# VectorE scales each image's last projection earlier; two ScalarE steps and one TensorE step change places

## What is computed

```python
xn = (x - mean) / jnp.sqrt(var + EPS) * g + b          # over the 64 channels
q, k, v = split(einsum('bchw,oc->bohw', xn, w_qkv))     # 8 heads of 32
q = q * scale
k = jax.nn.softmax(k, axis=-1)                          # over the 1024 pixels
context = jnp.einsum('bhcn,bhdn->bhcd', k, v)
out = jnp.einsum('bhcd,bhcn->bhdn', context, q)
x1 = einsum('bchw,oc->bohw', out, w_out) + b_out + xn

y = conv3x3(jnp.sign(x1), jnp.sign(W))                  # 64 to 64 channels
yn = (y - mean) * gamma / jnp.sqrt(var + BN_EPS) + beta # over all 8 images
result = yn + x1
```

## Time and profile before

| What | Value |
|---|---|
| median of 3 executions | 112.19 us (112.02 to 114.37) |
| the profiled execution | 112.12 us, its span 109.9 us |
| TensorE matmul busy | 76.6 us (70% of the span) |
| VectorE busy | 62.1 us (56%) |
| ScalarE busy | 53.5 us (49%) |
| GpSimd busy | 37.8 us (34%) |
| chain that ended last | PE 54%, DVE 14%, ACT 13%, issue 12% |
| mean granted TensorE clock | 0.934 of full speed |

### The profile page before, as it was taken

The page is one execution under the profiler, slowest core; times in us unless marked ns, Lnnn a source line. Parts: engine busy times, 40 slices in busy tenths (PEclk is TensorE's granted clock), DMA queues, the critical chain, the costliest instruction groups (busy, mean ns, idle before and its releaser), DMA issues.

```text
span 109.9 us, 2262 instructions
## 1 busy us (share of the span) xinstructions
PE 76.6 (70%) x855; PEld 44.3 (40%) x855; DVE 62.1 (56%) x134; ACT 53.5 (49%) x101; POOL 37.8 (34%) x49
## 2 busy tenths in 40 slices
PE   4999577776993997993980899666967999710000
PEld 4933145433551643553560556434625444310000
DVE  4516845966067148368379526935641629738900
ACT  0436569367577186291690038084171339349400
POOL 6000665602914206708539605706400000004410
PEclk9999999999999999999999679999999999995555
DMA  1999743900592000980002941061070081522893
GB/s 62 221 244 232 155 94 76 210 10 0 113 207 62 6 3 0 197 185 6 0 0 46 208 110 25 0 136 61 0 191 6 0 191 29 121 47 45 234 332 152
DMA packets 7565, 11.03 MB, mean 100 GB/s; under 512 B 1924, under 2 KB 4036, under 8 KB 7556
## 3 DMA queue, kind: packets, MB, share of 16 engines
q1 hardware_dynamic: 6164, 9.33, 37.1%
q0 software_dynamic: 336, 1.05, 2.8%
q10 hardware_dynamic: 1056, 0.52, 2.0%
HBM read 2.51 MB, written 2.10 MB: 42 GB/s over the span
## 4 chain that ended last, share of the span: by engine, by line
PE 54%; DVE 14%; ACT 13%; issue 12%; POOL 1%; ACTq 1%; POOLq 1%; DVEq 0%
PE ps L797 7%; PE ps L700 4%; PE ps L809 4%; PE ps L930 4%; PE ps L889 4%; ACT E L412 4%; PE ps L859 3%; PE ps L776 3%; DVE mx L556 3%; PE ps L878 3%; DVE E_lo L550 3%; DVE XN L537 2%; PE ps L815 2%; ACT lnv L361 2%; ACT rstd L367 2%
## 5 line engine op out<-in xcount | busy, mean ns | idle before, releaser
L556 DVE TENSOR_REDUCE mx<-ps 128x1 bf16<-128x1024 f32 x16 | 19.5, 1222 | 5.5 <-PE ps L754 5.5
L412 ACT ACTIVATE E<-ps 128x512 f32<-128x512 f32 x32 | 17.2, 590 | 4.8 <-PE ps L781 4.8
L309 POOL TENSOR_TENSOR E_lo<-E 128x512 bf16<-128x512 f32 x11 | 12.2, 1121 | 10.8 <-ACT E L412 10.8
L419 ACT COPY PT<-ps 128x256 f32<-128x256 f32 x8 | 3.0, 372 | 24.0 <-PE ps L815 15.6
L293 POOL TENSOR_SCALAR x_hi<-XN,hi_rows 128x512 bf16<-128x512 f32 x7 | 5.4, 766 | 21.2 <-DVE XN L537 21.2
L303 POOL TENSOR_TENSOR x_lo<-XN,x_hi 128x512 bf16<-128x512 f32 x8 | 9.2, 1154 | 9.4 <-DVE x_hi L578 8.9
L776 PE MATMUL ps<-wk_max,x_hi 64*128 64x256 bf16 x64 | 9.1, 275 | 2.4 <-ACT E L412 1.7
L561 DVE SCALAR_TENSOR_TENSOR wk_max<-ps,hi_rows,wk_hi 128x256 bf16<-128x256 f32 x8 | 3.9, 484 | 11.8 <-PE ps L761 11.7
L797 PE MATMUL ps<-E,XT 128*64 128x256 f32 x64 | 7.8, 384 | 3.7 <-issue 3.7
L336 POOL DMA_DIRECT2D out<-OUT x3 | 1.8, 614 | 22.9 <-DVE OUT L688 22.9
L779 PE MATMUL ps<-wk_lo,x_hi 64*128 64x256 bf16 x64 | 8.9, 269 | 0.0
(11 more groups left out here) (142 smaller groups left out, 152.6 us busy)
## 6 DMA issues: line engine op xcount, KB each, us to landing
X<-XN SPq DMA_DIRECT2D x16, 128.0 KB, 2.3
X<-in_x SPq DMA_DIRECT2D x4, 256.0 KB, 5.3
S<-x_hi SPq DMA_DIRECT2D x8, 128.0 KB, 2.4
S<-x_lo SPq DMA_DIRECT2D x8, 128.0 KB, 2.4
X<-X SPq DMA_DIRECT2D x4, 256.0 KB, 3.9
X<-X SPq DMA_DIRECT2D x8, 128.0 KB, 2.4
X<-in_x SPq DMA_DIRECT2D x6, 128.0 KB, 3.4
out<-OUT SPq DMA_DIRECT2D x3, 256.0 KB, 4.3
```

Source lines behind the costliest of these rows:

```text
L309: nc.gpsimd.tensor_tensor(e_lo, e, e_hi, ALU.subtract).then_inc(elo_pool, 1)
L412: nc.scalar.activation(E[:, b % 2, keys_of(j), :].rearrange("p k j -> p (k j)"), kt_ps[j % HALVES], ACT.Exp).then_inc(exp_ready, 1)
L556: nc.vector.tensor_reduce(mx[:, b % 2, t:t + 1], k_ps(b, t).rearrange("p a n -> p (a n)"), AX.X, ALU.max).then_inc(max_ready, 1)
```

## The change

It moves calls; no instruction is added, removed or resized.

- VectorE: in each round b from 2, `scale_r(b - 2)` stands first, ahead of `normalise(b + 2)`, `key_max(b + 1, 1)` and `split_exp(b - 1)`. It was behind them. After the loop, `scale_r(6)` stands ahead of `split_exp(7)`.
- ScalarE: in round 6 `signs(0)` stands behind `exp(6, 2)` and `exp(6, 3)`. In round 7 `signs(1)` stays ahead of its exponentials. `log_var(2)` and `inverse_std(2)` move from ahead of the loop to behind `exp(0, 1)`.
- TensorE: `variance(2)` moves from ahead of `max_rows(0)` to behind `shift_maxima(1, 0)` in round 0.

```diff
@@ scalar
             query_value_weights()
-            log_var(2)
-            inverse_std(2)
             for b in range(B):
                 exp(b, 0)
                 exp(b, 1)
                 if b == 0:
+                    log_var(2)
+                    inverse_std(2)
                     keep_xt(0)
...
-                if b == 7:
-                    signs(1, 0, 2)
-                exp(b, 2)
-                exp(b, 3)
                 if b + 3 < B:
@@ vector
             for b in range(B):
                 if b == 0:
                     key_max(1, 0)
+                if b >= 2:
+                    scale_r(b - 2)
                 if b + 2 < B:
                     normalise(b + 2)
...
                 if b > SPLIT:
                     split_exp(b - 1)
-                if b >= 2:
-                    scale_r(b - 2)
...
+            scale_r(LAST - 1)
             split_exp(LAST)
-            scale_r(LAST - 1)
             add_input(2, 0, 2)
@@ tensor
             make_query_value_weights()
-            variance(2)
             max_rows(0)
             for b in range(B):
                 keys_t(b, 0)
                 if b == 0:
                     shift_maxima(1, 0)
+                    variance(2)
                     transpose_x(0)
```

More of the change, by code:

```diff
@@ L445, in _ @@
                     tap_signs()
+                if b == 7:
+                    signs(1, 0, 2)
+                exp(b, 2)
+                exp(b, 3)
                 if b == 6:
```

## The result

| | before | changed |
|---|---|---|
| median of the executions | 112.11 us (4) | 101.02 us (4), 100.22 to 101.16 |
| ratio to before | | 0.8998 (95% interval 0.8938 to 0.9058) |
| span of the profiled execution | 109.9 us | 98.7 us |
| TensorE matmul busy | 76.6 us | 73.5 us |
| VectorE, ScalarE, GpSimd busy | 62.1, 53.5, 37.8 us | 62.0, 53.5, 37.7 us |

What follows compares the result with a forecast made beforehand. TensorE was taken to wait in six places for VectorE's `R`, ready but queued behind other work. Terms 0.36 + 3.70 + 3.42 + 1.03 + 0.36 + 0.66 + 1.18 = 10.71 took 112.12 to 101.4 us, range 100.3 to 104.2.

Steps and rivals of the forecast that it cites:

- What bounds the kernel: In six places TensorE waits for `R`, 0.45 us of VectorE work that stood ready behind other work.
- Rounds 2 and 4: TensorE's waits for `R` before the contexts of these rounds go: 1.85 us each, 3.70 us together.
- Round 5: Wait for `R` before `matrix(1)` goes, at full clock; `shift_maxima(7, 0)` starts at 61.98, not 65.40: 3.42 us.
- Round 6, round 7, last context: TensorE's waits before `split_context(5)`, `matrix(2)` and the last context go: 1.03, 0.66 and 1.18 us.
- Signs: Round 6, ScalarE: exponentials no longer stand behind the signs, whose part in the earlier keys of image 7 is 0.36 us.
- Front: Moving `variance(2)` brings `max_rows(0)` 1.33 us earlier and `XN` of image 2 0.36 us earlier, the gain counted.
- No change: Rival: something else coming in at the same time ended TensorE's waits; about 112 us, chance 0.03.
- Slower: Rival: VectorE's `scale_r` waits for a late projection and holds the normalisation chain; 118 us at 3.5 us lateness, chance 0.02.
- The clock falls anyway: Rival: low-clock spells on TensorE cost 1.3 us each; two or three give 102.7 to 105.3 us, chance 0.05.
- Another wait takes part of it back: Rival: slower two-input VectorE steps or late `mx` lose 1 to 3 us: 102.4 to 104.4 us, chance 0.10.

Runs made afterwards that it cites:

- the next step: Changed kernel with, in round 5 only, `split_exp(4)` ahead of `key_max(6, 1)` and `shift_keys(6)` ahead of `split_m(1)`: 100.94 us, ratio 0.8995.
- rounds 2 to 4 alone: Kernel before with `scale_r` first in rounds 2, 3 and 4 only: 108.72 us, ratio 0.9584.
- round 5 undone: Changed kernel with `scale_r(3)` alone back behind `split_exp(4)` in round 5: 104.67 us, ratio 0.9326.
- the run with the extra matmuls behind the wait: Changed kernel with `scale_r(3)` back behind `split_exp(4)`, plus ten constant matmuls in `matrix(1)` behind its wait for `R`: 106.85 us, ratio 0.9503.

## Why the prediction was right, step by step

- **What bounds the kernel.** Six waits for `R`, three of them not named in the chain. Taking them away with VectorE's edits alone gave 101.6 of the forecast 101.4: right. Reading 0.10 us between the end of `R` and TensorE's start, together with the wait in the code, was enough to name a releaser that the profile left out.
- **Rounds 2 and 4.** 3.70 forecast, 3.76 measured. `R` fits in VectorE's gap, and the maximum did not become the next wait.
- **Round 5.** 3.42 forecast, 3.41 measured, bounded as forecast by `E_lo` and its 1.61 us, with full clock. Its two parts, wait and clock, were shown separately. The wait left over was 1.07 where some 0.95 was said.
- **Round 6, round 7, last context.** 1.03, 0.66 and 1.18 forecast; 1.20, 0.72 and 1.10 measured, 2.87 against 3.02 in all; undoing them cost 3.0. The 0.17 more in round 6 is a matter of counting: the 1.03 ran from the end of the matmul before, and with the wait gone the context starts 0.17 before that end (61.22, against 61.17 + 0.22 = 61.39).
- **Signs.** 0.36 forecast, 0.34 in the traces, 0.39 when put back.
- **Front.** The one term that was off: 0.36 forecast, 0.16 measured. The mechanism held and the size of one step did not. The 0.71 + 0.62 = 1.33 by which everything behind the variance was to come earlier took the variance to the end of its last matmul, but `max_rows(0)` had started 0.46 after its first (15.88, 16.34). So the keys of image 0 came 1.15 earlier (17.19, and 15.51 + 0.53 = 16.04), and their exponentials with them. I let the rstd end 1.15 later. In the trace its logarithm starts at 17.34, right behind the two exponentials (16.37, 1.08 us). On the scale of before, 0.53 later, that is 17.87 and not 16.54, so 1.33 later, and `XN` with it. That the terms still add up to 10.7, as forecast, is luck to this extent: the 0.20 missing here is made good by the 0.17 of round 6.
- **Left out.** The start of TensorE, worth 0.5 between the two profiled executions. It made the sum of 10.7 come out as 11.2 in the spans. It belongs to the execution and not to the kernel, and I had left no room for it in the range.
- **The rivals.** "No change" fell with the two runs that moved `scale_r` alone (101.60) and everything but it (111.68). "Slower" was real one place further ahead only. "The clock falls anyway" did not come, granted clock 1.00 in all stretches of the loop. "Another wait takes part of it back" did not come in the changed kernel, and did come at once, by contention with GpSimd, when the next step was taken.

The range of 100.3 to 104.2 held the median of 101.02, near its lower end. One of the four executions, 100.22, lay just below it: the margin of 1.1 us below the forecast had no part for the start.

## What to carry to other kernels

Where a short step (0.45 us here) stands behind longer ones on its engine and another engine waits for it, place it in the first gap that begins after its own input is there: here that cost nothing, while one place further ahead its wait held up the queue and cost 4.7 us. Look for such waits also where the profile says "issue", by the end of the last instruction that the code's wait names. When a wait is removed, look at which instructions now run beside which: the next improvement was mostly lost to VectorE and GpSimd running beside each other and came back by moving one more step.

## What the runs showed of the hardware

- **VectorE beside GpSimd.** The same subtraction of 128x512 from two SBUF tensors took 0.68 us where it came first or GpSimd had nothing under way, and 0.88 to 1.61 where one of GpSimd's was under way. In the two long cases it ended some 0.55 us after GpSimd's instruction did, and so did the one of 1.14 in round 7 of the changed kernel (64.54 + 1.04 = 65.58, and 64.98 + 1.14 = 66.12), as if it had stood until that one was through. The Trainium skill says so (SBUF — State Buffer, the entry on the shared port pair among the terms: allocated by a lock and held for the whole instruction, the loser blocks). The traces agree. It goes the other way too: with VectorE first, GpSimd's `x_hi` took 1.14 us in place of 0.77.
- **TensorE's clock.** Idle gaps of 1.85 us did not lower it, one of 3.33 did, every time (the kernel before, without `scale_r`'s moves, rounds 2 to 4 alone, round 5 undone, and the run with the extra matmuls behind the wait). The fall to the lower level of 1.2 GHz came 0.5 to 0.6 us ahead of the restart in the last two and some 0.5 us behind it in the first three. Useless matmuls in the gap were worth 1.35 us.
- **TensorE's start.** The first eight matmuls of real work took 1.09 us in eight of the fourteen traces, and 1.16, 1.17, 1.36, 1.61, 1.83 and 1.95 in the others, of the same code and behind the same instructions, at a granted clock of 1.00 in all of them. That moves the whole kernel by up to 0.9 us from execution to execution, and is the limit of what a comparison of two profiled executions can tell unless starts are subtracted. What sets it stays open; it is not the granted clock.
